# Cross-attention and LoRA-MoE layer on one Trainium2 core: the second norm as one ScalarE block whose 32-row blocks are exchanged through DRAM

## What is computed

```python
n1 = layernorm(x)
scores = einsum('bsd,bmd->bsm', n1, ctx) / sqrt(D)
attn = softmax(where(mask[:, None, :], scores, -1e30))
x = x + where(any(mask), einsum('bsm,bmd->bsd', attn, ctx), 0)
n2 = layernorm(x)                       # the second norm
base = einsum('btd,od->bto', n2, weight)
probs = softmax(einsum('btd,ed->bte', n2, router_w))
vals, idx = top_k(probs, 2)             # vals divided by their sum
Ax = einsum('nd,erd->ner', n2, lora_A)
x = x + base + 2.0 * einsum('ner,ne,eor->no', Ax, w_dense, lora_B)
```

## Time and profile before

| | before |
|---|---|
| time, median of 3 runs | 1128.25 us (1128.23 to 1129.31) |
| span of the profiled execution | 1126.4 us |
| its own time | not listed apart from the span; the median of the runs is 1.85 us above the span |
| PE busy | 1067.7 us, 95% |
| DVE busy | 922.1 us, 82% |
| ACT busy | 709.8 us, 63% |
| POOL busy | 262.0 us, 23% |

### The profile page before, as it was taken

How to read it: one execution, slowest core, us unless ns; L and a number is a source line. 1 busy time by engine, 2 the same in 40 slices (tenths; PEclk the granted TensorE clock), 3 DMA queues, 4 the chain that set the end, 5 groups by cost and what they waited for, 6 DMA issues and landing times.

```text
span 1126.4 us, 20668 instructions
## 1 busy us (share of the span) xinstructions
PE 1067.7 (95%) x6160; PEld 1031.1 (92%) x6160; DVE 922.1 (82%) x2744; ACT 709.8 (63%) x1406; POOL 262.0 (23%) x286
## 2 busy tenths in 40 slices
PE   2699999999999999999999999999999999999998
PEld 2599999999999999999999999999999999999998
DVE  6988888888878888788878888788887888887874
ACT  5766765666766666666656667557666657756652
POOL 4522230222320232220322212222221222311200
PEclk9999999999999999999999999999999999999999
DMA  9222322412323312422213322223322323323200
GB/s 309 94 87 92 113 106 83 140 58 92 112 95 122 112 57 94 135 99 94 93 77 122 112 94 93 86 93 112 112 83 105 101 77 112 112 81 107 75 38 38
DMA packets 34588, 113.16 MB, mean 100 GB/s; under 512 B 4672, under 2 KB 7744, under 8 KB 34496
## 3 DMA queue, kind: packets, MB, share of 16 engines
q1 hardware_dynamic: 34496, 112.31, 29.2%
HBM read 78.74 MB, written 33.55 MB: 100 GB/s over the span
## 4 chain that ended last, share of the span: by engine, by line
PE 73%; DVE 16%; issue 8%; DMA 1%; ACT 1%; DVEq 0%; SPq 0%; POOL 0%; POOLq 0%
PE base_ps L767 21%; PE base_ps L769 20%; PE base_ps L768 20%; DVE xn L624 4%; PE ro_ps L806 3%; PE ro_ps L807 3%; PE s_ps L784 2%; PE s_ps L785 2%; DVE stats L563 2%; PE h_ps L829 1%; DVE x L610 1%; DMA w_raw<-in_wT 1%; DVE gate_b L674 1%; DVE h L679 1%; DVE top_at L652 1%
## 5 line engine op out<-in xcount | busy, mean ns | idle before, releaser
L457 ACT ACTIVATE xn<-x,shift,rstd 32x256 f32<-32x256 f32 x768 | 458.5, 597 | 262.5 <-POOL shift L374 244.1
L767 PE MATMUL base_ps<-w_hi,xT_hi 128*128 128x386 f32 (+1 forms) x1536 | 539.2, 351 | 1.5 <-DVE w_lo L278 1.4
L769 PE MATMUL base_ps<-w_hi,xT_lo 128*128 128x386 f32 (+1 forms) x1536 | 520.8, 339 | 0.0
L768 PE MATMUL base_ps<-w_lo,xT_hi 128*128 128x386 f32 (+1 forms) x1536 | 520.6, 339 | 0.0
L767 PEld LDWEIGHTS base_ps<-w_hi,xT_hi 128*128 128x128 f32 x1536 | 289.9, 189 | 9.7 <-issue 1.6
L768 PEld LDWEIGHTS base_ps<-w_lo,xT_hi 128*128 128x128 f32 x1536 | 290.5, 189 | 2.7
L769 PEld LDWEIGHTS base_ps<-w_hi,xT_lo 128*128 128x128 f32 x1536 | 289.8, 189 | 0.0
L360 POOL TENSOR_TENSOR rstd<-var_eps,neg_half 128x1 f32<-128x1 f32 x128 | 71.1, 555 | 820.1 <-DVE var_eps L568 820.1
L563 DVE BATCH_NORM_STATS2 stats<-x 128x6 f32<-128x512 f32 x256 | 164.1, 683 | 13.6 <-issue 11.4
L378 POOL TENSOR_TENSOR xT_lo<-xT_raw,xT_hi 128x1024 fp32r<-128x1024 f32 x62 | 147.4, 2398 | 0.0
L641 DVE TENSOR_TENSOR xT_lo<-x2T,xT_hi 128x512 fp32r<-128x512 f32 x128 | 82.7, 687 | 45.7 <-ACT xT_hi L463 45.7
(11 more groups left out here) (72 smaller groups left out, 985.9 us busy)
## 6 DMA issues: line engine op xcount, KB each, us to landing
xT_raw<-in_xT SPq DMA_DIRECT2D x64, 512.0 KB, 5.8
x<-in_x SPq DMA_DIRECT2D x64, 512.0 KB, 3.3
out<-x SPq DMA_DIRECT2D x64, 512.0 KB, 2.6
ctx_raw<-in_ctx SPq DMA_DIRECT2D x16, 256.0 KB, 4.8
w_raw<-in_wT SPq DMA_DIRECT2D x2, 1544.0 KB, 11.4
ctxT_raw<-in_ctxT SPq DMA_DIRECT2D x8, 256.0 KB, 4.5
w_raw<-in_wT SPq DMA_DIRECT2D x1, 1552.0 KB, 11.7
b_raw<-in_bT SPq DMA_DIRECT2D x1, 512.0 KB, 16.1
```

What stands on the lines that cost most here:

```text
L457: act.activation(xn2[a * QP:(a + 1) * QP, g, :], x[rows, slot(tile), a * DQ:(a + 1) * DQ], ACT.Identity, bias=shift2[rows, :], scale=rstd2 ...
L767: pe.matmul(out_, a_hi, w_h, start=start, stop=False, skip_group_check=again)
L768: pe.matmul(out_, a_hi, w_l, start=False, stop=False, skip_group_check=again)
L769: return pe.matmul(out_, a_lo, w_h, start=False, stop=stop, skip_group_check=again)
```

## The change

- The second norm is written by ACT alone, as one instruction of 128 x 1024 (`xn`), at the very start of ACT's step. DVE's four and ACT's twelve instructions of 32 x 256 go.
- The exchange of the 32-row blocks is done by DMA: SP stores `xn` to a scratch tensor `xn_dram` in DRAM (`xn_out`, 512 KB), waits until it has landed, and loads it back with four DMAs of 32 partitions x 4 x 256 (`xq_in`, 128 KB each) into `xq`.
- DVE's transposes are two of 128 x 512 in place of four of 128 x 256, one ahead of `softmax_split` and one behind it. They wait for all four loads.
- SP's step becomes: wait for `xn` of the tile two on and store it; wait for `out_done`, store the tile; wait for `xn_stored`, issue the four loads; in odd steps `load_xT` of the pair five tiles on; then the wait for the tile's store and `load_x`. The same pair was asked for at the beginning of the next step before.
- ACT's odd step has `xT_high` behind the norm; POOL's odd step has `norm1` between its two `xT_low`.
- PE's order: one chunk of group 2 stands ahead of `h_transpose`, then two chunks, `e_transpose`, two chunks, `readout`, three chunks, in even and odd steps alike.
- At the start: `b_raw` lies in the fourth slot of `x` and not in a tensor of its own, tile 3 is therefore loaded behind `b_split`; tile 2 is loaded earlier; the third weight group, `load_w(2)`, is issued behind the exchange of tile 0.

The diff, cut to its core:

```diff
+            def xn_out(tile):
+                sp.wait_ge(xn_done, count(tile, 1, 1))
+                sp.dma_start(xn_dram, xn[:, :]).then_inc(xn_stored, 16)
+
+            def xq_in(tile):
+                sp.wait_ge(xn_stored, count(tile, 16, 16))
+                for a in range(Q):
+                    sp.dma_start(xq[a * QP:(a + 1) * QP, :, :],
+                                 xn_dram[:, a * DQ:(a + 1) * DQ].rearrange("(g n) e -> n g e", n=QP))\
+                      .then_inc(xq_loaded, 16)
...
-            sp.dma_start(b_raw[:, :], bT_in).then_inc(b_loaded, 16)
+            sp.dma_start(b_raw, bT_in).then_inc(b_loaded, 16)
+            load_x((0, 2))
+            xn_out((0, 0))
+            xq_in((0, 0))
             sp.wait_ge(w_split[0], WPARTS)
             load_w(2)
-            load_x((0, 2))
+            sp.wait_ge(xT_split, 2)
+            load_xT((0, 4))
+            sp.wait_ge(b_split, 1)
             load_x((0, 3))
+            xn_out((0, 1))
+            xq_in((0, 1))
...
-                if j % 2 == 0 and exists(after(tile, 4)):
-                    sp.wait_ge(xT_split, pairs(tile, 2, 2))
-                    load_xT(after(tile, 4))
+                if exists(after(tile, 2)):
+                    xn_out(after(tile, 2))
                 sp.wait_ge(out_done, count(tile, G, FREE + G))
                 sp.dma_start(out[b * TPB + j], x[:, slot(tile), :]).then_inc(stored[slot(tile)], 16)
+                if exists(after(tile, 2)):
+                    xq_in(after(tile, 2))
+                if j % 2 == 1 and exists(after(tile, 5)):
+                    sp.wait_ge(xT_split, pairs(after(tile, 1), 2, 2))
+                    load_xT(after(tile, 5))
...
                 if j % 2 == 1 and exists(after(tile, 3)):
-                    for i in range(2):
-                        xT_low(after(tile, 3), i)
+                    xT_low(after(tile, 3), 0)
                 if exists(after(tile, 2)):
                     norm1(after(tile, 2))
+                if j % 2 == 1 and exists(after(tile, 3)):
+                    xT_low(after(tile, 3), 1)
...
-            def norm2(tile, g):
-
-                rows = slice(g * QP, (g + 1) * QP)
-                if g == 0:
-                    act.wait_ge(shift2_done, count(tile, 1, 1))
-                for a in range(DVE_Q, Q):
-                    act.activation(xn2[a * QP:(a + 1) * QP, g, :], x[rows, slot(tile), a * DQ:(a + 1) * DQ],
-                                   ACT.Identity, bias=shift2[rows, :], scale=rstd2[rows, :]).then_inc(xn2_act_done, 1)
+            def norm2(tile):
+                act.wait_ge(shift2_done, count(tile, 1, 1))
+                act.wait_ge(x2T_done, count(tile, TS))
+                act.activation(xn[:, :], x[:, slot(tile), :], ACT.Identity, bias=shift2[:, :],
+                               scale=rstd2[:, :]).then_inc(xn_done, 1)
...
             def step(tile):
                 b, j = tile
                 nxt, nxt2 = after(tile, 1), after(tile, 2)
+                if exists(nxt):
+                    norm2(nxt)
...
-                for g in range(Q):
-                    if exists(nxt):
-                        norm2(nxt, g)
-                    if g == 1:
-                        gate_exp(tile)
-                        if j % 2 == 0 and exists(nxt2):
-                            sT_copy(nxt2)
+                gate_exp(tile)
+                if j % 2 == 0 and exists(nxt2):
+                    sT_copy(nxt2)
...
+            def x2_transposes(tile, i):
+
+                dve.wait_ge(xq_loaded, count(tile, 16 * Q, 16 * Q))
+                out_ = x2T[:, :, :].rearrange("p c (g n) -> p g c n", n=QP)
+                dve.transpose(out_[:, i * QS:(i + 1) * QS],
+                              xq[:, i * QS:(i + 1) * QS, :].rearrange("p g (c n) -> p g c n", n=QP)).then_inc(x2T_done, 1)
...
                 router_top(tile)
-                if exists(nxt):
-                    norm2(nxt, 0)
-                    norm2(nxt, 1)
...
                 if exists(nxt):
-                    x2_transposes(nxt, range(Q - 1))
+                    x2_transposes(nxt, 0)
                 if exists(nxt2):
                     softmax_split(nxt2)
                 if exists(nxt):
-                    x2_transposes(nxt, range(Q - 1, Q))
+                    x2_transposes(nxt, 1)
...
+                base(tile, 2, range(1))
                 h_transpose(tile)
-                c = 2 if j % 2 == 0 else 5
-                base(tile, 2, range(c))
+                base(tile, 2, range(1, 3))
                 if exists(nxt2):
                     e_transpose(nxt2)
-                base(tile, 2, range(c, c + 2))
+                base(tile, 2, range(3, 5))
                 if exists(nxt2):
                     readout(nxt2)
-                base(tile, 2, range(c + 2, C))
+                base(tile, 2, range(5, C))
```

More of the change, by code:

```diff
@@ L116, in xattn_lora_moe_kernel @@
         w_raw = [sb(f"w_raw{i}", [P, C, GROUPS[0][1]]) for i in range(2)]
-        b_raw = sb("b_raw", [P, O])
         ctxT = sb("ctxT", [P, C, 2 * M], f32r)
@@ L131, in xattn_lora_moe_kernel @@
         x = sb("x", [P, XS, D])
-        xn2 = sb("xn2", [P, Q, D // Q])
+        b_raw = x[:, XS - 1, :]
+        xn = sb("xn", [P, D])
+        xq = sb("xq", [P, Q, DQ])
         xT_raw = sb("xT_raw", [P, 2, C, T2])
@@ L256, in xattn_lora_moe_kernel @@
         shift2_done = sem("shift2_done")
-        xn2_act_done = sem("xn2_act_done")
-        xn2_dve_done = sem("xn2_dve_done")
+        xn_done = sem("xn_done")
+        xn_stored = sem("xn_stored")
+        xq_loaded = sem("xq_loaded")
         x2T_done = sem("x2T_done")
@@ L518, in _ @@
                 xT_high((0, 2), i)
-            for g in range(Q):
-                norm2((0, 0), g)
-                if g == 1:
-                    softmax_exp((0, 1))
+            norm2((0, 0))
+            softmax_exp((0, 1))
             eT_copy((0, 1))
@@ L616, in norm2_stats @@
                 dve.tensor_scalar(neg_mean2[:, :], mean_var2[:, 0:1], -1.0, None, ALU.mult).then_inc(neg_mean2_done, 1)
-            def norm2(tile, g):
-                rows = slice(g * QP, (g + 1) * QP)
-                if g == 0:
-                    dve.wait_ge(rstd2_done, count(tile, 1, 1))
-                for a in range(DVE_Q):
-                    dve.tensor_scalar(xn2[a * QP:(a + 1) * QP, g, :], x[rows, slot(tile), a * DQ:(a + 1) * DQ],
-                                      mean_var2[rows, 0:1], rstd2[rows, :], ALU.subtract, ALU.mult)\
-                       .then_inc(xn2_dve_done, 1)
-            def x2_transposes(tile, quadrants):
-                for g in quadrants:
-                    dve.wait_ge(xn2_dve_done, count(tile, Q * DVE_Q, DVE_Q * (g + 1)))
-                    dve.wait_ge(xn2_act_done, count(tile, Q * ACT_Q, ACT_Q * (g + 1)))
-                    dve.transpose(x2T[:, :, g * QP:(g + 1) * QP], xn2[:, g, :].rearrange("p (c n) -> p c n", n=QP))\
-                       .then_inc(x2T_done, 1)
+            def x2_transposes(tile, i):
[3 more added lines that the diff above has]
+                              xq[:, i * QS:(i + 1) * QS, :].rearrange("p g (c n) -> p g c n", n=QP)).then_inc(x2T_done, 1)
             def x2T_low(tile):
@@ L746, in _ @@
             softmax_scores((0, 1))
-            for g in range(Q):
-                norm2((0, 0), g)
             softmax_split((0, 1))
-            x2_transposes((0, 0), range(Q))
+            for i in range(TS):
+                x2_transposes((0, 0), i)
             x2T_low((0, 0))
@@ L921 @@
     out = nc.dram_tensor("out", (B * S // P, P, O), mb.dt.float32, kind="ExternalOutput").ap()
-    xattn_lora_moe_kernel(nc, *args, out)
+    xn_dram = nc.dram_tensor("xn_dram", (P, D), mb.dt.float32, kind="Internal").ap()
+    xattn_lora_moe_kernel(nc, *args, xn_dram, out)
     r = run_bass_kernel_spmd(nc, [{f"in_{n}": a for n, a in arrays.items()}], core_ids=[0])
```

16 lines of the change are left out of this document (6 added, 10 removed).

## The result

| | before | after |
|---|---|---|
| time, median | 1128.38 us (1128.23 to 1129.31, 4 runs) | **1139.42 us** (1137.96 to 1141.84, 4 runs) |
| ratio | | 1.0093, 95% interval 1.0077 to 1.011 |
| span of the profiled execution | 1126.4 us | 1140.1 us (its own time 1141.84) |

The account below looks back on a forecast made before the run. PE, busy 95% of the span, was taken as the bound, so only its waits counted: 1126.4 - 20.7 (router) - 5.6 (start) + 3 (exchange) = 1103.1 us span, plus 1.85 to the median: 1105 us, range 1098 to 1132.

Parts of the forecast that it names:

- Item 1: Router: h ready 0.85 to 1.7 us sooner, one chunk ahead of its transpose; PE's wait for h goes, -20.7 us.
- Item 5: SP's queue and side effects: later tile store, moved input loads, POOL's second xT_low behind norm1; nobody waits, no cost.
- Item 3: Exchange through DRAM: store lets loads start after 2.81 us, loads take 3.85 us to the transposes (bounds 3.05 to 6.1).
- Item 2: Second norm as one ACT instruction of 128 x 1024: 1.24 us (bounds 1.05 to 2.4), replacing twelve pieces.
- Item 4: PE's wait for the exchange at e_split: odd-step margin 0.1 to 0.3 us, charged +3 us.
- Item 6: Start, tile 0: earlier norm and exchange, loads landed near 32.8, the 2.9 us wait for h gone; -5.6 us.
- A: Rival: exchange half a microsecond longer, PE waits for e_split in odd steps; 1118 us (1110 to 1124), chance 0.21.
- B: Rival: exchange becomes the bound through DVE's own loop, from loads of about 4.9 us on; slower than before, chance 0.16.

Follow-up runs that it names:

- e1: Kernel after, with ACT's two xT_high again ahead of the norm and POOL's two xT_low ahead of norm1: 1121.71 us.
- e12: Kernel after with ACT's order alone put back (xT_high ahead of the norm), POOL's norm1 still between its two xT_low: 1122.37 us.
- e8: Kernel before, without exchange, with POOL's two xT_low of an odd step moved behind norm1: 1236.83 us.
- e4: Kernel before with one chunk of group 2 put ahead of h_transpose, nothing else: 1113.41 us.
- e13: e1 (all four loads on SP) with the tile's 512 KB store issued behind the loads of xq: 1105.68 us.
- e3: e1 with two of the four xq loads issued from ACT's queue behind gate_exp: 1109.1 us.
- e5: e3 (two queues) with the tile's 512 KB store issued behind the loads of xq: 1091.64 us.
- e6: e3 with softmax_split put ahead of both of DVE's transposes: 1090.7 us.
- e10: e1 (one queue, tile's store ahead of the loads) with softmax_split put ahead of the transposes: 1099.5 us.
- e14: e13 (one queue, tile's store behind the loads) with softmax_split put ahead of the transposes: 1091.65 us.
- e9: e5 (two queues, tile's store behind the loads) with softmax_split put ahead of the transposes: 1092.12 us.
- e7: e1 with each load bringing one group of 32 rows to all 128 partitions, each transpose waiting for its own two loads: 1343.56 us.

## Why the prediction was wrong, point by point

- **Item 1, the router: the step that failed first.** "On ACT ... now there is one norm and, in odd steps, two casts ..., together about the same, so `gate_exp` comes no later" is true of ACT's sum. What the order did to POOL was not asked: its pair starts with the first cast, and was moved from ahead of `gate_a` onto it. Item 5 even looked at POOL's `xT_low` and wrote "nobody waits, no cost". e1 and e12 price that at 17 to 18 us of the 34 between forecast and result; e8 shows the mechanism without any exchange. The other 17 are item 3's. The other half of item 1 held: e4 alone gains 15 us, and in e1 the wait for `h` is gone.
- **Item 2, the norm's price:** 1246 ns against 1.24 us forecast. Right.
- **Item 3, the exchange: the right chain, with the loads too short.** The store was 2.67 to 3.13 for 2.81. The loads were 4.67 in the mean for 3.85. The forecast let a quarter of a 512 KB load land after 2.25 us and added 0.3 for which it had no row; the median to landing is 3.0, and the slowest between 600 and 740 us had 3.8. In e13, with the tile's store behind them, the loads still took 4.45, so most of the excess is that of a small load itself. The tile's store, named there as "part of the upper side", added 0.2 to 0.4 us, and that alone cost 16 us (e1 against e13). The four issues were in the forecast, with 1.3 us; what was not seen is that moving half of them to a second queue takes 0.3 to 0.4 us off (e3, e5). By the figures that the prediction took from the Trainium skill (DMA: Bandwidth & Descriptors, Anatomy of one DMA) the store takes an estimated 3.2 us and the last load 2.3; the measured 2.67 to 3.13 and 3.0 decide, and that section gives its fit for DMAs issued by GpSimd, where these are issued by SP. The one larger load that the same page's rules ask for, as the prediction quotes them from the Trainium skill, was not tried.
- **Item 4, does PE wait for it: the mechanism was right**, the place too (`e_split` behind DVE's transposes), as e6, e10 and e14 show by moving it. The slope can be read from the square: from e3 to e5 the mean load time over all waits falls by 0.35 us (4.41 to 4.06) and the time by 17.5, from e1 to e3 by 0.30 us and 12.6, from e1 to e13 by 0.26 us and 16.0, from e13 to e5 by 0.39 us and 14.0. That is 36 to 62 us per us, between the 32 and the 64 that were forecast for one step in two and for every step. The level was too high: e5, with loads of 4.0 to 4.2, gives 1091.6, where the forecast expected 1102 or more. Its floor of 33.15 us a pair was PE's busy time of before, and the pairs of e9 take 32.8 (131.35 us a batch). So the sum held two errors of opposite sign, a floor about 10 us too high and loads too short. In the kernel after DVE's waits for the exchange came in even steps, not in the odd ones that the forecast named: in odd steps DVE came to the transposes late, from the collision.
- **Item 5**, SP's queue: the input's loads cost nothing visible, but the tile's store ahead of the loads did, 16 us.
- **Item 6, the start:** 2.0 us won for 5.6. The store went out at 27.53, as forecast. It was given only the time of its data there, landing near 29, and not the 2.81 us of item 3; the loads began at 30.97. They took 4.45 us to the transposes at 35.42, where the forecast had 32.8: 2.0 us of the 2.6 are the store's, 0.6 the loads'.
- **The rivals.** A and B had the exchange's part: e1, with the order mended, is A (1121.7 for 1118). Against B's argument, "they stood behind 512 KB of x", stands that the loads of `xq` have the tile's store beside them in every step. B's end came true by A's exchange and the collision together, and the collision was among no rival; that B's sum for loads of 5.0 us gives 1139, the time that was measured, is chance.

The Trainium skill has a rule that speaks against this order and was not weighed: its page SBUF — State Buffer (section SBUF: two separate sides) says that VectorE in its two-port modes and GpSimd use one shared pair of ports, and that the one which starts first holds it for its whole instruction while the other stands. The trace agrees: `gate_a` began at 617.36, 0.11 us behind POOL's second subtraction, took 2.31 us beside POOL's 2.39 and ended with it. In which mode VectorE ran it no trace shows.

## What to carry to other kernels

When one engine's order changes, look at which instruction of a third engine it releases, and what that one then runs beside; here POOL's 2.39 us against DVE's tiny instructions cost 17.7 us, while the 374 us of work taken from ACT gained nothing by themselves. A transfer put on the path is to be priced with what else is issued just before and behind it, and the first thing to try is whether the waiting engine has anything urgent behind the wait: e10 moved one small group and got 22 us, more than the second queue or the store's place. The best kernel here is e6 (1090.7 us, 3.4% less than before), but e14 gives the same within 1 us from changes of order alone: one queue, ACT's casts ahead of the norm, the tile's store behind the loads and `softmax_split` ahead of the transposes. How much of that needs the exchange is open: e4 has none and is at 1113.4 us, and no run puts further edits of order into the kernel before.

## What the runs showed that was not expected

- POOL blocks DVE only in some instructions, and how long they are does not decide it. Beside POOL's subtraction, in e5 (POOL from 617.13 to 621.90):

```profile
617.13 4.77 POOL L403 TENSOR_TENSOR xT_lo<-xT_raw,xT_hi 128x1024 fp32r<-128x1024 f32 x2
617.46 1.28 DVE L591 BATCH_NORM_STATS2 stats<-x 128x6 f32<-128x512 f32 x2
619.13 0.15 DVE L596 TENSOR_SCALAR var_eps<-mean_var 128x1 f32<-128x1 f32 x1
620.86 1.07 DVE L670 CAST top_at<-top_at 128x2 f32<-128x2 uint32 x1
```

  Statistics and a `tensor_scalar` of one element a partition run at full pace; the cast of two elements stands until POOL ends. So do `tensor_scalar` of 8 elements and of 256 (in the kernel after and in e8, above).
- PE's busy time hides stalls. With 6160 matmuls in each, PE is busy 1073.2 us in the kernel after and 1060.1 in e9, and in the same 136 us e14 has 799 matmuls where the kernel after has 767. Idle time alone (4.2 us of 136, or 3%) understates a gain of 4%.
- The way in which a load is cut decides its rate: with the four blocks of 32 partitions as the slowest dimension of the source 4.5 of 16 engines were at work and 94 GB/s moved, with 32 partitions at a time 13.4 engines and 269 GB/s (e7 and e1).
